# The last feed-forward part put into attention's queues

## The reference

```
x = x + 0.5 * ffn(layernorm(x))
x = x + attention(layernorm(x))      # 16 heads, a gated delta rule over 512 steps, output product Wo
x = x + 0.5 * ffn(layernorm(x))      # same ffn weights
ffn(z) = ((silu(z @ Wg * gs) * (z @ Wu * us)) @ Wd) * ds      # 256 -> 768 -> 256, weights rounded to fp8
```

## Time and profile before

| | us |
|---|---|
| median of 3 runs | 2474.54 (2473.37 to 2475.38) |
| the profiled execution | 2475.66 |
| its span, first to last instruction | 2473.9 |
| PE busy in the span | 2355.2 (95%) |
| DVE, ACT, POOL busy | 2017.3, 1813.7, 1824.8 |

### The profile page before, as it was taken

One profiled execution on the slowest core, in us unless ns is written; L12 is line 12 of the kernel. 1 busy time (PEld: TensorE's weight loads), 2 busy tenths in 40 slices (PEclk: granted clock), 3 DMA queues, 4 the chain that ended last, 5 costly groups with the idle time before them and its releaser, 6 DMA issues. The chain is left out here.

```text
span 2473.9 us, 64148 instructions
## 1 busy us (share of the span) xinstructions
PE 2355.2 (95%) x24496; PEld 1825.3 (74%) x24496; DVE 2017.3 (82%) x4246; ACT 1813.7 (73%) x3567; POOL 1824.8 (74%) x1977
## 2 busy tenths in 40 slices
PE   4897899999999999999999999999999999998598
PEld 2553588888888888888888888888888878877365
DVE  7775888888888888888888888888888888886353
ACT  3673677777777777777777777777777777776364
POOL 4783577777777777777777877777777787777365
PEclk9998999999999999999999999999999999999699
DMA  6241011111121111111211111112211111111001
GB/s 165 91 144 43 27 32 32 30 27 30 31 57 49 31 32 31 32 32 32 52 52 30 32 32 32 32 31 49 54 30 29 31 32 32 32 32 23 22 32 38
DMA packets 72833, 103.59 MB, mean 42 GB/s; under 512 B 21456, under 2 KB 33744, under 8 KB 72400
## 3 DMA queue, kind: packets, MB, share of 16 engines
q1 hardware_dynamic: 72528, 99.48, 15.9%
HBM read 85.69 MB, written 13.77 MB: 40 GB/s over the span
## 5 line engine op out<-in xcount | busy, mean ns | idle before, releaser
L1598 PE MATMUL a_bank<-k_z,k_kqv 128*128 128x512 f16 x2304 | 598.9, 380 | 9.8 <-DVE a_qb L1173 3.8
L1287 ACT ACTIVATE a_inv<-a_bank 128x512 f16<-128x512 f32 x640 | 383.3, 599 | 207.0 <-PE a_bank L1447 191.2
L1104 DVE TENSOR_TENSOR k_y<-a_bank,k_masks 128x256 f16<-128x256 f32 x768 | 318.8, 415 | 126.0 <-PE a_bank L1433 122.0
L941 POOL TENSOR_TENSOR k_diag<-k_ident,k_bcol 128x512 f32<-128x512 f32 x128 | 132.9, 1038 | 228.7 <-DVE a_prod L1080 213.7
L1598 PEld LDWEIGHTS a_bank<-k_z,k_kqv 128*128 128x128 f16 x2304 | 198.1, 98 | 139.7 <-DVE a_kb L1173 5.9
L1173 DVE SCALAR_TENSOR_TENSOR a_kb<-a_bank,k_prm,a_kb 128x511 f32<-128x511 f32 (+2 forms) x384 | 283.1, 737 | 14.9 <-ACT a_kb L1231 14.4
L1173 DVE SCALAR_TENSOR_TENSOR a_vb<-a_bank,k_prm,a_vb 128x511 f32<-128x511 f32 (+2 forms) x384 | 283.9, 739 | 0.1
L1173 DVE SCALAR_TENSOR_TENSOR a_qb<-a_bank,k_prm,a_qb 128x511 f32<-128x511 f32 (+2 forms) x384 | 282.8, 737 | 0.4
L1447 PE MATMUL a_bank<-a_inv,k_y 128*128 128x64 f16 x3072 | 271.4, 192 | 1.0 <-DVE k_y L1104 1.0
L1445 PE MATMUL a_bank<-k_y,a_inv 128*128 128x64 f16 x2560 | 236.0, 193 | 4.8 <-DVE k_y L1104 2.2
L1433 PEld LDWEIGHTS a_bank<-a_inv,a_am 128*128 128x128 f16 x3072 | 168.1, 98 | 94.4 <-ACT a_inv L1287 5.6
(11 more groups left out here) (152 smaller groups left out, 6696.7 us busy)
## 6 DMA issues: line engine op xcount, KB each, us to landing
a_decay<-decay_rows SPq DMA_DIRECT2D x128, 258.0 KB, 3.8
a_cum<-cumulative_rows SPq DMA_DIRECT2D x96, 258.0 KB, 3.6
weight_pairs<-f_pairs SPq DMA_DIRECT2D x15, 512.0 KB, 2.9
k_kqv<-weight_pairs SPq DMA_DIRECT2D x9, 512.0 KB, 4.7
stream<-in_L_attn_x SPq DMA_DIRECT2D x8, 512.0 KB, 6.8
out<-stream SPq DMA_DIRECT2D x8, 512.0 KB, 2.9
f_raw<-in_L_attn_Wk SPq DMA_DIRECT2D x4, 512.0 KB, 4.8
f_raw<-in_L_attn_Wq SPq DMA_DIRECT2D x4, 512.0 KB, 5.0
```

The costliest lines, as they stand in the source:

```text
L1104: nc.vector.tensor_tensor(even(y16[:, j], mb), bank[LEV[par]][:, 0:U * C // 2].rearrange("p (u b m) -> p u b m", u=U, m=mb), masks[:, j].r ...
L1287: nc.scalar.activation(both, bank[LEV[par]][:, :].rearrange("p (two b m) -> p two b m", two=2, m=mb), ACT.Copy).then_inc(m[f"act_lev{par}" ...
L1598: mm = pe.matmul(bank[PJ[j % 2]][:, :], wt, z16[:, zh, k, cols], start=(x == 0), stop=(x == 5))
```

## The change

The phase for the third part is gone; `ffn_phase` becomes `first_phase` (the first part alone, unchanged), and the third part's operations stand in attention's queues. Buffers of attention that are dead by then hold its data: the saved weights go where the normalised tokens of batches 0 to 2 were (`z16`), `ztok` and `sg` into the v buffer of the even sequences, the hidden values into the k and q buffers (six instead of three), `scaled` into q, the scale row into the gate buffer. SP loads the weights at s = 106 and the scale row behind the last step.

Steps up to 124 are as before. On every engine, operations of batches 0 and 1 are put between and into the last ones: DVE has `stats2(0)` before step 124 and `stats2(1)` before step 125, POOL `root2(0)` and `root2(1)` there, ACT `z_normed(0)` before step 125. Steps 125 to 127 are `tail(s)`, with `gate_up(x)` (gate and up products of block x, counted over batches) in place of the projections, x = 0 to 3 in step 126 and 4 to 7 in step 127; z_turned, z_high and z_low of batches 0 and 1 stand in tails 125 and 126. Then attention's last operations and blocks 8 to 11 and downs 0 to 5 alternate, and `turn(b)` for b = 1 to 7 has the downs of batch b and the gate and up products of batch b+1. Gate has one bank (`PJ[0]`) and up one (`PJ[1]`); `down_b` are the two level banks.

The core of the diff:

```diff
+            for s in range(-8, STEPS - 4):         # gpsimd
                 step(s)
+            nc.gpsimd.memset(eps[:, :], EPS).then_inc(f["pool_eps"], 1)
+            pool.wait_ge(f["pool_eps"], 1)
+            root2(0)
+            step(STEPS - 4)
+            root2(1)
+            for s in range(STEPS - 3, STEPS):
+                tail(s)
...
+            def tail(s):                           # gpsimd
+                x = 4 * (s - STEPS + 2)
+                system_low(s)
+                one(s + 2, 1)
+                state(s - 1)
+                hidden_low(x - 2)
+                one(s + 1, 2)
+                strengths(s + 2)
+                scaled_q(s - 1)
+                hidden_low(x - 1)
+                gated(s - 2)
+                one(s + 2, 0)
+                system16(s + 1)
+                first_inverse(s + 1)
+                root(s - 1)
+                low(s - 2)
+                hidden_low(x)
+                one(s + 2, 3)
+                scaled_k(s)
+                hidden_low(x + 1)
...
+            def tail(s):                           # vector
+                x = 4 * (s - STEPS + 2)
+                corrected(s - 1)
+                system(s + 1)
+                if s == STEPS - 2:
+                    z_low(1)
+                hidden(x - 1)
+                level(s, 3)
+                hidden(x)
+                statistics(s - 1)
+                aggregated(s - 1)
+                level(s, 4)
+                if s == STEPS - 3:
+                    z_low(0)
+                hidden(x + 1)
+                mixing(s + 1)
...
+            for s in range(-8, STEPS - 4):         # vector
                 step(s)
-            dve.wait_ge(m["dve_out"], STEPS)
+            stats2(0)
+            step(STEPS - 4)
+            stats2(1)
+            for s in range(STEPS - 3, STEPS):
+                tail(s)
...
+            def tail(s):                           # scalar
+                x = 4 * (s - STEPS + 2)
+                affine(s - 2)
+                if s == STEPS - 2:
+                    z_high(1)
+                hidden_gate(x - 1)
+                gate(s + 2, 2)
+                level(s, 2)
+                gate(s + 2, 3)
+                hidden_high(x - 2)
+                hidden_high(x - 1)
+                hidden_gate(x)
+                level(s, 3)
+                high(s - 2)
+                hidden_high(x)
+                hidden_gate(x + 1)
+                first_inverse(s + 1)
+                level(s, 4)
+                if s == STEPS - 3:
+                    z_high(0)
+                normed(s - 1)
+                level(s + 1, 0)
+                hidden_high(x + 1)
+                hidden_gate(x + 2)
+                if s == STEPS - 3:
+                    z_normed(1)
+                kdecayed(s + 1)
+                level(s, 5)
...
+            def gate_up(x):                        # tensor
+
+                if not 0 <= x < MT * B:
+                    return
+                b, j = divmod(x, MT)
+                if x == 0:
+                    pe.wait_ge(f["dma_weights"], 48)
+                if j == 0:
+                    pe.wait_ge(f["act_zh"], KT * max(b + 1, 2))
+                    pe.wait_ge(f["dve_zl"], KT * max(b + 1, 2))
+                need(pe, f["act_silu"], x)
+                products(bank[PJ[0]], fgate16, x, f["pe_gate"])
+                need(pe, f["dve_hidden"], x)
+                products(bank[PJ[1]], fup16, x, f["pe_up"])
...
+            correction(STEPS - 1)                  # tensor, behind the tails
+            down(0)
+            read(STEPS - 1, 0, U // 2)
+            read(STEPS - 1, U // 2, U)
+            down(1)
+            gate_up(8)
+            output(STEPS - 2)
+            down(2)
+            gate_up(9)
+            out_turned(STEPS - 1)
+            down(3)
+            gate_up(10)
+            down(4)
+            output(STEPS - 1)
+            gate_up(11)
+            down(5)
+            z_turned(2)
+            for b in range(1, B):
+                turn(b)
...
+            def turn(b):                           # tensor
+                x = MT * b
+                for j in range(MT):
+                    down(x + j)
+                    gate_up(x + MT + j)
+                    if j == 2:
+                        z_turned(b + 2)
```

More of the change, by code:

```diff
@@ new lines, in _ @@
+            root2(0)
[3 more added lines that the diff above has]
+                tail(s)
+            scaled_q(STEPS - 1)
+            gated(STEPS - 2)
+            low(STEPS - 2)
+            root(STEPS - 1)
+            hidden_low(6)
+            hidden_low(7)
+            hidden_low(8)
+            gated(STEPS - 1)
+            low(STEPS - 1)
+            root2(2)
+            hidden_low(9)
+            hidden_low(10)
+            hidden_low(11)
@@ L1213, in _ @@
+            corrected(STEPS - 1)
+            hidden(7)
+            statistics(STEPS - 1)
+            aggregated(STEPS - 1)
+            hidden(8)
+            output(STEPS - 2)
+            stats2(2)
+            hidden(9)
+            scales()
+            hidden(10)
+            output(STEPS - 1)
+            hidden(11)
+            down_scaled(0)
+            z_low(2)
+            stats2(3)
+            for b in range(1, B):
+                turn(b)
         @block.scalar
@@ new lines, in _ @@
+            for s in range(-8, STEPS - 3):
+                step(s)
+            z_normed(0)
+            for s in range(STEPS - 3, STEPS):
+                tail(s)
+            affine(STEPS - 2)
+            hidden_gate(7)
+            high(STEPS - 2)
+            hidden_high(6)
+            hidden_high(7)
+            hidden_gate(8)
+            normed(STEPS - 1)
+            hidden_high(8)
+            hidden_gate(9)
+            hidden_high(9)
+            affine(STEPS - 1)
+            hidden_gate(10)
@@ L1362, in _ @@
+            high(STEPS - 1)
+            hidden_high(10)
+            z_normed(2)
+            hidden_gate(11)
+            hidden_high(11)
+            z_high(2)
+            for b in range(1, B):
+                turn(b)
         @block.tensor
@@ new lines, in tail @@
+            def tail(s):
+                x = 4 * (s - STEPS + 2)
+                level_b(s, 2)
+                gram_k(s + 1)
+                correction(s - 1)
+                gate_up(x)
+                level_a(s, 3)
+                read(s - 1, 0, U // 2)
+                read(s - 1, U // 2, U)
+                level_b(s, 3)
+                if s == STEPS - 3:
+                    z_turned(0)
+                gate_up(x + 1)
+                level_a(s, 4)
+                first_inverse(s + 1)
+                gram_q(s + 1)
+                update(s - 1)
+                level_b(s, 4)
+                level_a(s + 1, 0)
+                gate_up(x + 2)
+                k_turned(s + 1)
+                level_b(s + 1, 0)
+                level_a(s, 5)
+                output(s - 2)
+                level_b(s, 5)
+                level_a(s + 1, 1)
+                v_turned(s)
+                state_k(s)
+                if s == STEPS - 3:
+                    z_turned(1)
+                level_b(s + 1, 1)
+                out_turned(s - 1)
+                first_solution(s)
+                gate_up(x + 3)
+                level_a(s + 1, 2)
+                check_solution(s)
```

595 lines of the change are left out of this document (381 added, 214 removed).

## The result

| | before | changed |
|---|---|---|
| median, us | 2474.59 (2473.37 to 2475.99, 8 runs) | 2468.05 (2465.78 to 2469.5, 8 runs) |
| ratio | | 0.9974, 95% interval 0.9965 to 0.9982 |
| profiled execution, its span | 2475.66, 2473.9 | 2468.06, 2466.3 |

The change gains 6.5 us. I had forecast 13.5 (2461): the sign was right and the time lies in the range, but the gain is half of the forecast. The changed kernel measured again later ("e7") gave 2467.64 (2466.17 to 2470.39, 10 runs), 6.9 less than the kernel before beside it, so 6.5 to 7 is firm.

What follows compares the result with a forecast made beforehand. TensorE, busy 95% of the span, was taken as the bound. Steps, drain and turns put the last down at 2449.3; plus 6.6 gives 2455.9, plus 5 for clock a span of 2461; median forecast 2461, range 2438 to 2475.

Steps and rivals of the forecast that it cites:

- Ceiling: From 2250.7 to the end: 36.2 us idle, 6 half clock, 2 hole ahead of last down; gain about 44, to 2432.
- Step 124: GpSimd's root2(0) waits for VectorE's stats2(0), delaying scaled_q and PE's read(123): 5.1 us lost, bounds 0 and 6.2.
- Step 125: Queue waits for affine 1.9, first_inverse 5.5, k_turned 3.4, first_solution about 1.3: 10 us more.
- Waits from step 126 on: PE waits: gate_up(0) 2.7, level_b 1.5 and 1.3, up(4) 1.1, read(126) 0.5; drain 4.3; first turn 1.1.
- PE's own work: Priced at back-to-back pitches: step 126 10.9 plus 6.9, step 127 7.9 plus 6.9, drain 19.0, turns 102.3 us.
- Clock: Slower clock behind new waits of 5, 5.5, 3.4 and 2.7 us: three spells taken, 5 us, bounds 0 and 6.8.
- From span to median: Span 2461 plus 1.8 gives an execution of 2462.7; median 1.1 below that, 2461.6, stated as 2461.
- A: Rival: queue orders don't bind because slack ahead of 2236 absorbs them; 2432, or 2447 with half the waits; chance 0.20.
- B: Rival: turns slower because gate and up have one bank each; 2483 at 0.6 us a pair; chance 0.07.
- C: Rival: clock stays lower through the tail; 2481 with a third at half speed, 2469 with a sixth; chance 0.15.
- the pairs in the tails: Four gate/up pairs each in steps 126 and 127, 6.9 us of work; steps forecast at 22.4 and 18.2 us.

Runs made afterwards that it cites:

- e7: The changed kernel measured again with no edit: 2467.64 us, ratio 0.9973.
- e4: Changed kernel plus 83 useless PE products ahead of four long waits (read(123), first_inverse(126), k_turned(126), gate_up(0)), nothing else moved: 2461.53 us, ratio 0.9951.
- e1: Changed kernel with only VectorE's stats2(0) moved earlier, from the seam of steps 123 and 124 into step 120 behind mixing: 2461.56 us, ratio 0.9948.
- e2: Changed kernel with only GpSimd's root2(1) moved later, from ahead of tail 125 to behind first_inverse(126) in it: 2461.30 us, ratio 0.9947.
- e3: Changed kernel with only VectorE's z_low(0) moved later in tail 125, from ahead of mixing(126) to behind new_state(124): 2465.55 us, ratio 0.9963.
- e5: Changed kernel with stats2(0) earlier, root2(1) and z_low(0) later, and ScalarE's z_normed(0) moved behind gate(127,3) in tail 125: 2447.50 us, ratio 0.9894.
- e6: Changed kernel with the eight gate/up pairs taken out of tails 126 and 127 and put in a row right behind them: 2467.63 us, ratio 0.9973.
- e9: The kernel with four moves (e5), with PE's gate_up(0) in tail 126 put behind the read of chunk 125 and level_b: 2447.36 us, ratio 0.9887.

## Why the prediction was half right

The mechanism was right, wait by wait; two terms of the sum were too small. The prediction's marks, set against the traces (us; the forecast column has no clock in it, and e4 measures just that):

| stretch on PE | forecast | changed | e7 | e4, clock kept |
|---|---|---|---|---|
| gram_k(125) to gram_k(127) | 45.9 | 50.5 | 52.1 | 46.3 |
| to the correction of 126 | 22.4 | 25.0 | 25.0 | 23.3 |
| to the correction of 127 | 18.2 | 18.9 | 18.9 | 18.9 |
| to gate_up(12) | 23.3 | 23.9 | 24.9 | 23.9 |
| to the end of the last down | 103.4 | 104.0 | 104.0 | 104.0 |
| sum | 213.2 | 222.3 | 224.9 | 216.5 |

- *Ceiling, 44 us.* Right in kind: the seam, the barrier and the hole ahead of the last down are gone. The last product of before ended at 2467.27 and that of the changed kernel at 2459.65, both 6.6 ahead of the end.
- *Step 124, 5.1.* Measured wait 5.07, released by GpSimd's scaled_q, through system_low and strengths, as written. e1 shows that it is the cause. (The upper bound of 6.2 was a slip: 2247.4 less 2241.45 is 5.95.)
- *Step 125, 10.* The waits forecast as 1.9, 5.5 (in two parts, as it turned out: 1.36 and 3.87) and 3.4 were 1.65, 5.2 and 3.47; e2 and e3 show the last two, and e5, with z_normed(0) moved too, is free of the first. The 1.3 forecast for first_solution was 0.40.
- *Waits from step 126 on.* gate_up(0) 2.67 for 2.7; level_b 1.55 and 1.21 for 1.5 and 1.3; up(4) 0.58 for 1.1; read 0.47 for 0.5; output(127) 2.09 for 0.9; down(6) 1.52 for 1.6; gate_up(12) 0.69 for 0.9. By stretch, length less busy time in the stage rows above, PE stood still for 4.6, 3.4, 4.3 and 1.4 us; the forecast had 4.6, 3.4, 4.3 and 1.1. In the drain that is luck: 1.2 too little at output(127) and 0.9 of small waits that never came.
- *PE's own work, the first step that failed: 2.5 us too small.* It was priced at the pitch of back-to-back products: 17.8, 14.8, 19.0 and 102.3 us. Busy were 18.7 (20.3 less the 1.6 by which e4 is shorter there), 15.5, 19.6 and 102.6. The prediction saw the reason, "the drain behind the last product of every stretch", and left it out of the sum. Eight down products follow one another at 0.87 us but take 1.04 to the end of the last, so every wait begins 0.17 later than the pitch says; by my estimate the eleven waits from step 126 to gate_up(12) make 1.9 of the 2.5. Steps 124 and 125 add 0.4 (e4's 46.3 against 45.9).
- *Clock, the second step that failed: 5 us taken, 6.5 measured.* I took three spells of 1.7 between bounds of 0 and 6.8. Against e4 it was 5.8 in the changed kernel's trace, 8.4 in that of e7 (1.0 of it in the drain), 6.5 by the medians. The spells run into one another in step 125: its row has 0.75 of the clock over 27.4 us. A spell at half speed was read rightly, though 2.02 against 0.87 compares a length to the end with a pitch (from start to start it is 1.82 against 0.95). But I sized it by a step in which only short waits stood, though the seam had waits of the new length, and the row of that stretch has clock 0.60:

```profile
2305.00 0.40 PE L1578 MATMUL a_bank<-k_wo,a_oh 128*128 128x256 f16 x1 [4.30 <-POOL a_ol L1045]
...
2312.70 0.40 PE L1578 MATMUL a_bank<-k_wo,a_oh 128*128 128x256 f16 x1 [4.10 <-POOL a_ol L1045]
```

- *Start.* gram_k(125) stands at 2237.39 where the sum began at 2236.15, 1.2 later, at equal code: at the 407-us mark it is 1.3. e7, which starts 0.35 earlier than the kernel before, shows that this is scatter.
- *From span to median.* I took 1.1 off because the profiled execution of the kernel before stood that much above its median, and rounded 0.6 away. The changed kernel's profiled execution stands at its median, so 1.7 us of the forecast had nothing under them.

For the profiled execution the terms add up: start 1.2, clock 0.8, own work and the rest of the stretches 3.3, span to median 1.7, together the 7.0 us by which the forecast was too good. Four of them are of the mechanism and three are scatter and rounding. The forecast was a difference of two large numbers, 44 gained and 30 given back, so that small errors halved what is left.

Of the rivals, A (all covered) was excluded by the 5.07; B (one bank each for gate and up) as well, since batch follows batch at 16.47 (z_turned at 2397.18, 2413.65, 2430.12), the same as in the earlier trace rows, and the clock stays at 1.00. C was right in part: spells from 2240 to 2296 at a lower clock, and in some executions one more in the drain (e7, 0.87 over 13 us). The Trainium skill ("TensorE: Matmul & The Clock Gate", section "A second HAM failure mode: psum-queue depth-cycling") tells of a clock that swings where PE idles briefly and often between groups of products that cycle through banks. The turns don't show it, at 1.00 over 104 us; but PE was busy for 102.6 of them, so they hardly test it.

One belief was right only in part: I priced the pairs in the tails by the rule that they fill waits (22.4 and 18.2, of which 11.3 more than before for 13.8 of work). e6 shows that the changed kernel gained nothing by it, since each pair brings a wait of its own there: PE for z_low(1), VectorE's level behind a hidden value, GpSimd's scaled_q behind a low half. With the first of these waits filled (e9) the pairs cost 11.7.

## What to carry to other kernels

- An operation put into an in-order queue costs what stands behind it, not its own length: look at when its input is ready, not at how busy the engine is. Two roots on an engine that is busy for three quarters of the time cost 6.5 and 6.8 us here (e1, e2), the slower clock behind the waits included, and moving the one's input earlier and the other later gave it back.
- Filling a gap only pays if the filler's own input is ready there. The same eight pairs cost 14.7 us with one of them in a place where it waited, and 11.7 with that one moved (e6, e7, e9). Try it the other way round too, all in a row behind, before believing in the fill.
- Where PE waits several us more than once, count the clock with the waits, and from a row with waits of that length. Work priced at the pitch of back-to-back products lacks the end of the last product ahead of every wait, 0.17 us each here.

## What the runs showed of the hardware

- 83 useless products on PE made the kernel 6.5 us faster, 0.26%, by keeping the granted clock at its upper level over waits of 2.7 to 5 us (e4).
- Behind the same wait of 2.1 us, ahead of output(127), the granted clock over 13 us was 1.00 in five traces and 0.87 in five others, once each for the very same kernel. It is worth 1.0 us.
- The same first part, in executions of kernels that share its code, reached the same scan at 404.56 to 408.17 us in eleven profiled executions. So two profiled executions can differ by that much before the edited part begins.
